# Three spare bf16 matmuls behind every edge-tile sum of a four-layer graph network

## The reference

```python
h = relu(layernorm(x)); x = x + L0(h, ...)   # hyperbolic: messages weighted by distances
h = relu(layernorm(x)); x = x + L1(h, ...)   # softmax over the edges of a target
h = relu(layernorm(x)); x = x + L2(h, ...)   # exp(-leaky_relu(s_src + s_dst)) as weight
h = relu(layernorm(x)); x = x + L3(h, ...)   # plain mean over the edges of a target
# each of them holds:
agg = segment_sum(coef[:, None] * h[src], dst, num_segments=N)
```

## Time and profile before

| | us |
|---|---|
| median of 3 runs | 5282.82 (5278.07 to 5283.91) |
| the profiled execution's own time | 5278.94 |
| its span, first to last instruction | 5277.1 |
| busy: PE / DVE / ACT / POOL | 3291.6 / 3440.5 / 1850.3 / 3348.5 |
| busy share: PE / DVE / ACT / POOL | 62% / 65% / 35% / 63% |
| mean granted clock of PE | 0.805 of 2.4 GHz |

### The profile page before, as it was taken

How to read it: one execution, slowest core, us unless ns; L and a number is a source line. 1 busy time by engine, 2 the same in 40 slices (tenths; PEclk the granted TensorE clock), 3 DMA queues, 4 the chain that set the end, 5 groups by cost and what they waited for, 6 DMA issues and landing times. The chain is left out here.

```text
span 5277.1 us, 59132 instructions
## 1 busy us (share of the span) xinstructions
PE 3291.6 (62%) x11741; PEld 2264.1 (43%) x11741; DVE 3440.5 (65%) x10607; ACT 1850.3 (35%) x4402; POOL 3348.5 (63%) x3529
## 2 busy tenths in 40 slices
PE   3388887888543566566564566656662566666667
PEld 2266665666332333333333344434441344444445
DVE  4299999999994666666667555555557455555555
ACT  0555555555684333333335333333336000000001
POOL 0377777777004777777761777777771677777773
PEclk8599999999776777777877888888886777777788
DMA  2454555554114444444435555555554544444443
GB/s 79 113 132 133 133 133 133 135 133 119 49 35 127 107 107 107 107 107 107 107 86 168 131 134 134 132 131 134 134 132 142 138 114 113 114 113 114 106 107 99
DMA packets 302414, 617.14 MB, mean 117 GB/s; under 512 B 66553, under 2 KB 175093, under 8 KB 302070
## 3 DMA queue, kind: packets, MB, share of 16 engines
q0 software_dynamic: 168960, 467.01, 33.9%
q1 hardware_dynamic: 107766, 117.55, 7.4%
q10 hardware_dynamic: 25344, 28.85, 2.1%
HBM read 560.58 MB, written 52.57 MB: 116 GB/s over the span
## 5 line engine op out<-in xcount | busy, mean ns | idle before, releaser
L457 POOL DMA_INDIRECT X<-table,src_tab x2640 | 2499.3, 947 | 1396.4 <-issue 752.7
L562 PE MATMUL psum<-X,onehot 128*128 128x259 f32 x5280 | 1824.7, 489 | 1001.1 <-ACT onehot L699 326.2
L1106 DVE SCALAR_TENSOR_TENSOR A<-A,same_tab,psum 128x259 f32 x3476 | 1670.4, 481 | 799.9 <-PE psum L562 564.3
L562 PEld LDWEIGHTS psum<-X,onehot 128*128 128x128 f32 x5280 | 1162.3, 239 | 1459.2 <-ACT onehot L699 562.1
L447 POOL DMA_INDIRECT X<-table,src_tab x880 | 836.9, 951 | 348.3 <-issue 251.3
L699 ACT ACTIVATE onehot<-G,zero_col,ecols 128x128 f32<-128x128 bf16 x1760 | 727.0, 481 | 701.0 <-PE psum L562 460.2
L571 PE MATMUL psum<-H,G 128*128 x1760 | 605.4, 431 | 314.2 <-DVE G L1194 195.5
L551 PE MATMUL psum<-X,onehot 128*128 128x259 f32 x1760 | 568.4, 408 | 4.3 <-DVE A L1106 2.2
L571 PEld LDWEIGHTS psum<-H,G 128*128 128x128 f32 x1760 | 326.5, 207 | 491.2 <-issue 451.8
L699 ACT ACTIVATE onehot<-onehot,zero_col,coef 128x128 f32<-128x128 bf16 x880 | 365.8, 481 | 128.3 <-DVE coef L1237 107.0
L1194 DVE SCALAR_TENSOR_TENSOR G<-psum,X 128x257 f32<-128x257 f32 x880 | 365.7, 417 | 64.0 <-DMA X<-table,src_tab 39.7
(11 more groups left out here) (324 smaller groups left out, 2863.4 us busy)
## 6 DMA issues: line engine op xcount, KB each, us to landing
X<-table,src_tab POOLq DMA_INDIRECT x3520, 2.8
plain<-rows_dram SPq DMA_DIRECT2D x110, 256.0 KB, 3.5
plain<-rows_dram ACTq DMA_DIRECT2D x176, 160.0 KB, 3.5
table<-H SPq DMA_DIRECT2D x21, 906.5 KB, 7.7
x_dram<-X SPq DMA_DIRECT2D x21, 896.0 KB, 4.2
X<-x_dram SPq DMA_DIRECT2D x14, 896.0 KB, 11.2
X<-in_x SPq DMA_DIRECT2D x2, 6144.0 KB
table<-H SPq DMA_DIRECT2D x1, 6345.5 KB, 27.2
```

The source lines that it names most:

```text
L457: pool.indirect_dma_start(ring[:, s % SLOTS, :], None, table, bass.IndirectOffsetOnAxis(src_tab[:, s:s + 1], 0)).then_inc(sem(f"batch_in{s ...
L562: pe.matmul(psum[:, k % ACC_BANKS, 0:W], hots[:, k % HOTS, :], ring[:, k, :], start=True, stop=True).then_inc(sem("used"), 1)
L1106: stt(total, total, same, psum[:, t % ACC_BANKS, 0:W], ALU.mult, ALU.add).then_inc(sem("sum_added"), 1)
```

## The change

Behind each fp32 sum of the second and third pass PE gets three more matmuls, and behind each of the fourth pass two. Each multiplies the 128x128 identity in bf16 (`ident_b`, made in the set-up and not used so far) by the same identity read four times over (512 columns), and writes a whole PSUM bank that nobody reads: bank 5 in the second pass, bank 7 in the third and fourth. They wait for no semaphore and count up none. So that bank 5 is free in the second pass, the two transposes of `turn_ends` write to the end of bank 7, and DVE's two scans in `row_links` read from there.

```diff
@@ sum_step(q, i, k) @@
                 pe.matmul(psum[:, k % ACC_BANKS, 0:W], hots[:, k % HOTS, :], ring[:, k, :],
                           start=True, stop=True).then_inc(sem("used"), 1)
+                for _ in range(2 if q == 2 else 3):
+                    pe.matmul(psum[:, 5 if q == 0 else 7, :], ident_b[:, :],
+                              ident_b[:, :].rearrange("p (o e) -> p o e", o=1).to_broadcast([P, 4, P]), start=True, stop=True)
@@ turn_ends(n) @@
-                pe.transpose(psum[0:1, 5, 0:GR], run_max[:, P - 1:P], ident[0:GR, 0:GR])
-                pe.transpose(psum[0:1, 5, GR:2 * GR], back_max[:, 0:1], ident[0:GR, 0:GR]).then_inc(sem("ends_t"), 1)
+                pe.transpose(psum[0:1, 7, 3 * P:3 * P + GR], run_max[:, P - 1:P], ident[0:GR, 0:GR])
+                pe.transpose(psum[0:1, 7, 3 * P + GR:3 * P + 2 * GR], back_max[:, 0:1], ident[0:GR, 0:GR]).then_inc(sem("ends_t"), 1)
@@ row_links(i, h) @@
                 dve.tensor_tensor_scan(back_row[:, 0:GR][:, ::-1], no_back[:, bass.ds(s0, GR)],
-                                       psum[0:1, 5, GR:2 * GR][:, ::-1], -BIG, ALU.add, ALU.max)
-                chain(dve.tensor_tensor_scan(run_row[:, 1:GR + 1], no_pass[:, bass.ds(s0, GR)], psum[0:1, 5, 0:GR],
+                                       psum[0:1, 7, 3 * P + GR:3 * P + 2 * GR][:, ::-1], -BIG, ALU.add, ALU.max)
+                chain(dve.tensor_tensor_scan(run_row[:, 1:GR + 1], no_pass[:, bass.ds(s0, GR)], psum[0:1, 7, 3 * P:3 * P + GR],
                                              run_row[:, 0:1], ALU.add, ALU.max))
```

## The result

| | before | after |
|---|---|---|
| median of 7 runs, us | 5282.82 (5277.62 to 5284.15) | 5302.12 (5297.43 to 5308.64) |
| the profiled execution's own time | 5278.94 | 5306.63 |
| its span | 5277.1 | 5304.8 |
| mean granted clock of PE | 0.805 | 0.929 |

The change makes the kernel 0.4% slower: ratio 1.004, 95% interval 1.0028 to 1.0051. That is 19.3 us between the medians. The three passes and the stretches between them tell where these 27.7 us are.

A forecast was written before the change was run, and what follows sets the result against it. Gathers every 1.25 us were taken to bound the passes and hide the extras; the three pass ends add 10 + 7.5 + 2 = 19.5 us to 5282.8, giving 5302 us, range 5285 to 5335.

The forecast's parts named there:

- The pace of the passes: Within the passes: a gather starts every 1.25 us, POOL's pause stays 0.305 us, and POOL never waits for PE.
- The price of an extra: Each added 512-column matmul on PE: 0.215 us at the full clock, 0.43 at the low one.
- A step of 1.09 us: PE in second and third pass: a sum of 0.44 us plus three extras of 0.65.
- own scores at 0.28 us a batch: Third pass: four batches a group cost 1.1 us in all, against 3.0 at the sequencer-paced 0.76 each.
- rival A: Third pass: PE becomes the bound from 25.0 us a group; 5362 us, or 5330 with half of that; chance 0.14.
- rival C: Not slower, around 5288 us: ends under 10.6 us, by matmuls at 0.17 us or a warm clock; chance 0.14.
- The small matmuls of the second pass: Between the sums of a group: at most 0.18 us at five places, 0.9 in all; PE's group 22.6 of 25.0.
- PE's idle time ahead of a landing: Second and third pass: idle time before a group's rows land falls to about 2 us but not to nothing.
- The clock: Inside the passes: granted clock above 0.9 in second and third; a dip costs 1.7 us a group and still fits.
- The ends: From last landing to last add, PE paces: 10, 7.5 and 2 us more in second, third and fourth pass.
- B: Clock stays low despite busy PE: a step costs 2.2 us, the two passes 1640 us more; chance 0.02.
- D: Whole kernel faster by over 0.2%, which needs gathers closer together than 1.25 us; chance 0.04.

The follow-up runs named there:

- e9: The change without extras behind the last 31, 20 and 5 sums, against the kernel before: 5289.37 us against 5289.66, ratio 1.0001.
- e8: The whole change run again unaltered, for a second profile of the gathers' pace: 5296.07 us in its one run.
- e11: No extras behind the last 31, 20, 5 sums; eight more just ahead in third and fourth pass; against the kernel before: 5289.77 us against 5289.66, ratio 0.9999.
- e1: The change without extras behind the last 31, 20 and 5 sums, on the slower chip, against the kernel before: 6218.00 us against 6088.08, ratio 1.0219.

## Why the prediction was right

The forecast was 5302 us, the result 5302.12. The mechanism is the one that was forecast; that the two numbers meet to 0.1 us is luck, since single terms are off by up to 1.7 us and one of them lies outside its own bounds. Point by point:

- **The pace of the passes.** Right: 0.305 us of pause after, whoever is named, and e9 has no measurable cost with 98% of the extras in place.
- **The price of an extra, 0.215 us.** Right. The view of the line says 379 ns for one, and three in sequence are shown as 0.81 us, so (0.81 - 0.38) / 2 = 0.215. The timeline of PE in the third pass after shows it with the rest of that step:

```profile
L565 PE MATMUL psum<-ident_b x7040: 377/379/634, 1678.7 to 5241.8; 128*128 128x512 bf16 x196
```

```profile
3023.80 0.81 PE L565 MATMUL psum<-ident_b 128*128 128x512 bf16 x3
3026.01 0.70 PE L562 MATMUL psum<-X,onehot 128*128 128x259 f32 x2 [1.40 <-ACT onehot L702]
...
3029.36 0.60 PE L562 MATMUL psum<-X,onehot 128*128 128x259 f32 x2
3029.80 0.81 PE L565 MATMUL psum<-ident_b 128*128 128x512 bf16 x3
3030.45 0.60 PE L562 MATMUL psum<-X,onehot 128*128 128x259 f32 x2
3030.89 0.81 PE L565 MATMUL psum<-ident_b 128*128 128x512 bf16 x3
3031.53 0.44 PE L596 MATMUL psum<-wide_rows,onehot 128*128 x5
```

- **A step of 1.09 us, and own scores at 0.28 us a batch in the third pass.** Right: 3029.36 to 3030.45, and 0.44 for five, as when they stood ready in the queue. Sequencer-paced batches of 0.76, rival A's ground, are nearly gone: 156 of the 176 batches take 0.44. The 81 ns of the Trainium skill ("TensorE: Matmul & The Clock Gate", section "Back-to-back issue gap"), weighed in the prediction, are for 128 columns, and five of 128 columns in 0.44 us speak against them here as before. The same sentence of that section gives about 131 ns for 512 columns, which the prediction left out and which would have spoken for rival C, not for A. This trace shows 0.215 for 512 columns, and the measurement decides: weight loads of 98 ns cost nothing beyond the columns.
- **The small matmuls of the second pass.** Too low: 0.9 us a group was taken from one of the five places, with 0.18. The group's median is 25.06 us with 1.52 idle, so PE needs 23.5, not 22.6, and 23.5 - 21.7 = 1.8 us are the small matmuls'. The group still fits, so nothing came of it inside the pass.
- **PE's idle time ahead of a landing** falls from 7.50 to 1.40 us in the group of the third pass that is shown (1.7 in the median of its groups); 2 had been forecast. In the second pass the median is 1.52. DVE's idle time ahead of a landing is 158.1 / 44 = 3.6 us in the second pass and 182.5 / 44 = 4.1 in the third, in the mean, more than the 2 that had been named for it too.
- **The clock.** Behind the start of the second and third pass it is 1.00 until the last gather. The dips that I had allowed for (1.7 us a group) did not come in any group of theirs, though PE is idle once in each, for 0.5 to 1.6 us in the second pass and 1.0 to 2.3 in the third. One came at the last landing of the second pass, after 2.31 us of idle time: the first three extras take 1.49 us there instead of 0.81.
- **The ends.** 11.7, 6.0 and 0.9 us against 10, 7.5 and 2: the sum of 18.6 comes near the 19.5 because errors of opposite sign cancel. The second pass's 11.7 lies above the high end that had been given for it (10.9): from the last landing (2749.87) to the last add it takes 37.7 us, not the 35 named as a sign. One dip of the clock is in it, as the high end allows (1.7), and the rest fits the small matmuls, which were put at 0.8. In the third pass I had expected the low clock at the start, and the first sum shows 0.70 us, the full one; without it the forecast was 5.7. In e8 the low clock is there, and the same end is 7.5 us longer than before, so that this term differs from run to run.
- **The rivals.** A: four extras are needed for it, not three. B is out by the granted clock. C's second way, that a full clock gives time back, is worth under 2 us at the ends by e11 and nothing in the stretches between the passes. Its threshold of 0.17 us a matmul was worked out from 6.5 us; the sum lies 19.5 - 10.6 = 8.9 above 10.6, which makes it 0.16, still further from 0.215. D is out by the pause.
- **What it missed** is that the cover differs from chip to chip. The passes hide the extras where gathers keep coming every 1.25 us; on the chip whose PE completions show late they cost 2% (e1).

## What to carry to other kernels

Work that is hidden in a steady loop is not hidden at the loop's end: count the items that are left when the bounding engine (here the gathers) has stopped, and multiply them with what the next engine now needs above the one that paced them before. Keeping TensorE's clock up gains nothing while another engine sets the pace; it is worth at most what PE's own time on the path falls by, and DVE's 0.62 us a step may take that over at once. Filling PE to 91% also gives away the slack that catches up late steps; the one chip whose completions show late paid 130 us for it.

## What the runs showed of the hardware that I had not expected

One of the three chips of the experiments runs the unchanged kernel at 6088 us instead of 5281 and 5290, with the same durations of single gathers and adds (0.946 and 0.48 us) but with DVE and POOL released up to several us behind the ends that the records of the sums show. The distance between two gathers has two values, 1.251 and 1.254 us, one for a whole execution (0.946 and 0.949 us for the gather itself), which moves the time of this kernel by some 10 us (an estimate: 3520 x 0.003) whatever its code. And a granted clock of 1.00 held through the second and third pass with one pause in every 25 us, of 1.5 and 1.7 us in the median and up to 2.3; at other places a fall to 0.50 came after a pause of 1.97 (e8) or 2.31 us, so the length of the pause alone doesn't tell it.
